# TensorE signals once in each attention step, at the scores, instead of several times; ten buffers for the one-hot matrices instead of six

## What is computed

```python
s_i = relu(einsum('bthd,bsd->bths', q_i, k_i))       # 4 index heads
I = einsum('bths,h->bts', s_i, idx_w)
I = where(local, inf, I); I = where(causal, -inf, I)   # the last 64 keys always
_, idx = top_k(I, 96)
key_c, value, kr_sel = ...[bi, idx]                    # 96 keys for each query
scores = (q_c . key_c + q_r . key_r) * scale           # 8 heads
out = softmax(scores) . value @ W_out
```

## Time and profile before

| what | us |
| --- | --- |
| median of three timed runs (939.28 to 943.36) | 941.9 |
| span of the profiled execution | 1199.2 |
| TensorE busy in the span | 913.6 |
| VectorE busy | 679.3 |
| ScalarE busy | 509.0 |
| GpSimd busy | 480.2 |
| chain that ended last: TensorE / another core or unknown queue / VectorE / issue / ScalarE | 46% / 20% / 13% / 10% / 8% |

### The profile page before, as it was taken

The page is one execution under the profiler, slowest core; times in us unless marked ns, Lnnn a source line. Parts: engine busy times, 40 slices in busy tenths (PEclk is TensorE's granted clock), DMA queues, the critical chain, the costliest instruction groups (busy, mean ns, idle before and its releaser), DMA issues.

```text
span 1199.2 us, 17728 instructions
## 1 busy us (share of the span) xinstructions
PE 913.6 (76%) x5742; PEld 520.4 (43%) x5742; DVE 679.3 (57%) x1979; ACT 509.0 (42%) x1463; POOL 480.2 (40%) x738
## 2 busy tenths in 40 slices
PE   6699749289479796879676794875749897888885
PEld 3345415145245453536343352443426582343353
DVE  3788628067158466549474473884403314968763
ACT  5456315044136464547354372643416332423420
POOL 3600562712711777573717427156560104411020
PEclk8668859679579788879687697885859998988987
DMA  8101211101100111110101001001070251000000
GB/s 232 34 1 25 43 26 38 29 20 33 29 19 5 25 26 23 21 23 16 23 11 22 19 12 23 11 17 25 16 188 21 69 139 31 1 1 10 0 10 18
DMA packets 59642, 39.98 MB, mean 33 GB/s; under 512 B 27072, under 2 KB 51360, under 8 KB 59424
## 3 DMA queue, kind: packets, MB, share of 16 engines
q1 hardware_dynamic: 44064, 23.40, 7.6%
q0 software_dynamic: 12800, 14.15, 5.8%
q10 hardware_dynamic: 2688, 1.31, 0.4%
HBM read 33.31 MB, written 5.55 MB: 32 GB/s over the span
## 4 chain that ended last, share of the span: by engine, by line
PE 46%; another core or an unknown queue 20%; DVE 13%; issue 10%; ACT 8%; DMA 1%; POOL 1%; SPq 0%; DVEq 0%; ACTq 0%; POOLq 0%
PE psI L655 5%; PE psK L745 5%; PE psK L641 4%; PE psS L1753 3%; PE psP L807 3%; PE psP L814 2%; PE psS L781 2%; PE psK L733 2%; ACT R L903 2%; PE psP L796 2%; PE psS L784 2%; DVE SC L1115 2%; PE psP L641 2%; DVE G L1971 1%
## 5 line engine op out<-in xcount | busy, mean ns | idle before, releaser
L621 POOL DMA_INDIRECT G<-key_rows,idx x284 | 276.2, 973 | 349.0 <-DVEq L1142 247.8
L1031 ACT ACTIVATE PT<-psP 128x256 f32<-128x256 f32 x128 | 48.7, 380 | 360.1 <-remote 270.3
L1311 DVE CUSTOM_DVE_ANT_0 S<-psS,cst 128x208 f32<-128x208 f32 x128 | 47.4, 370 | 262.9 <-remote 225.2
L655 PE MATMUL psI<-kiT,qiT 64*128 64x512 f32 (+5 forms) x320 | 108.3, 697 | 74.1 <-ACT R L903 57.1
L641 PE MATMUL psK<-cst 128*128 128x512 bf16 x315 | 101.4, 437 | 6.3 <-issue 6.3
L781 PE MATMUL psS<-KT,Q 96*32 96x128 f32 x1024 | 64.8, 305 | 27.9 <-remote 17.5
L1115 DVE SCALAR_TENSOR_TENSOR SC<-R,w_i,SC 128x512 f32<-128x512 f32 (+5 forms) x120 | 78.5, 654 | 5.5 <-ACT R L903 1.9
L1145 DVE MAX8 top<-SC 128x8 f32<-128x128 f32 (+15 forms) x64 | 78.5, 1226 | 2.3
L1007 ACT ACTIVATE KT<-psK 96x512 f32<-96x512 f32 x96 | 56.7, 591 | 51.9 <-remote 26.4
L903 ACT ACTIVATE R<-psI 128x512 f32<-128x512 f32 (+5 forms) x160 | 73.3, 510 | 12.2 <-PE psI L655 6.0
L1147 DVE FIND_INDEX8 idxf<-top,SC 128x8 uint32<-128x128 f32 (+15 forms) x64 | 78.2, 1223 | 0.0
(11 more groups left out here) (348 smaller groups left out, 1889.1 us busy)
## 6 DMA issues: line engine op xcount, KB each, us to landing
G<-key_rows,idx POOLq DMA_INDIRECT x284
rtmp<-idx_rows SPq DMA_DIRECT2D x32, 128.0 KB
xslots<-zrow SPq DMA_DIRECT2D x4, 320.0 KB, 9.0
SC<-xslots SPq DMA_DIRECT2D x8, 160.0 KB
yslots<-SC ACTq DMA_DIRECT2D x8, 160.0 KB, 2.7
V<-val_rows SPq DMA_DIRECT2D x15, 80.0 KB
xr<-in_x SPq DMA_DIRECT2D x1, 1024.0 KB, 9.3
qiT<-in_w_gate SPq DMA_DIRECT2D x4, 256.0 KB
```

Source lines behind the costliest of these rows:

```text
L621: pool.indirect_dma_start(ring[o % RING][:, g % GPB, DR:], None, key_rows, bass.IndirectOffsetOnAxis(ap=idx[:, t, g:g + 1], axis=0),).then ...
L655: pe.matmul(psI[i][:, 0:w], lhs, kiT[64 * i:64 * i + 64, CH * c:CH * c + w], start=True, stop=True).then_inc(s["i_mm"], 1)
```

## The change

One semaphore, `pe_step`, takes the place of thirteen in the loop. TensorE raises it once a step, on the last matmul of `scores(n-1)` (or of `out_project`, where a step has one). `through(n)` is the count after step n, and all readers on ScalarE, VectorE, GpSimd and SyncE wait for the count of the step in which their matmuls stand. What stood at the end of a step (`tail`: index pair, query, router) now runs at the start of the next one, after the signal, and is covered by the signal of that next step. `out_project(t)` moves from ahead of the scores of step 8(t+2) to the end of step 8(t+2)-1, and waits for `s_min` and `vs_cp` there in place of the wait for `s_y_mm`. `one_hot` gets four more buffers, in the half of `ot_region` that `OT` leaves free, and `key_match` waits once a block, for the end of the step of the block before the last, not for single key tiles.

```diff
-NVS, NOH = 7, 6
+NVS, NOH = 7, 10
...
+        def tail_of(n):
+
+            return (n in index_pairs or n in Q_AT or n in QT_AT or n == LAST_Y
+                    or any(n in TILE_AT[stage] for stage in ("x1_t", "router", "cumulate")))
+
+        counted = [n for n in range(N0, N1 + 1) if tail_of(n - 1) or 0 <= n < NT * NB + LAG_W]
+
+        def through(n):
+
+            return sum(1 for m in counted if m <= n)
...
-                    if b == NB - 1 and t >= 1:
-                        out_project(t - 1)
-                        pe.wait_ge(s["y_mm"], t)
...
-                for n in range(N0, N1):
-                    st, b = divmod(n, NB)
-                    keep_warm(psK, WARM_TAIL.get(n - NT * NB, 0))
+                for n in range(N0, N1 + 1):
+                    mm = tail(n - 1)
+                    if n < N1:
+                        keep_warm(psK, WARM_TAIL.get(n - NT * NB, 0))
                     if 0 <= n - LAG_T < NT * NB:
-                        p_transpose(n - LAG_T)
+                        mm = p_transpose(n - LAG_T)
                     if 0 <= n - LAG_W < NT * NB:
-                        weighted(n - LAG_W)
+                        mm = weighted(n - LAG_W)
                     if n == 1:
                         rank_transpose()
                     if 0 <= n < NT * NB:
-                        front(n)
+                        mm = front(n)
                     if 0 <= n - LAG_S < NT * NB:
-                        scores(n - LAG_S)
+                        mm = scores(n - LAG_S)
+                    if n in Y_AT:
+                        pe.wait_ge(s["s_min"], n - 1)
+                        if (n - 4) // NB in ONE_HOT:
+                            pe.wait_ge(s["vs_cp"], hot_order(n - 4) + 1)
+                        mm = out_project(Y_AT[n])
+                    if n in counted:
+                        mm.then_inc(s["pe_step"], 1)
...
                 def k_copy(n):
                     if n // NB in ONE_HOT:
                         return
-                    act.wait_ge(s["k_t"], ring_order(n) + 1)
-                    if n >= 2:
-                        act.wait_ge(s["s_mm"], n - 1)
+                    act.wait_ge(s["pe_step"], through(n))
...
                 def p_copy(n):
-                    act.wait_ge(s["p_t"], n + 1)
-                    if n >= 1:
-                        act.wait_ge(s["pv"], n)
+                    act.wait_ge(s["pe_step"], through(n + LAG_T))
...
                 def o_copy(n):
                     t, b = divmod(n, NB)
-                    act.wait_ge(s["pv"], n + 1)
+                    act.wait_ge(s["pe_step"], through(n + LAG_W))
...
+                    if m >= 2:
+                        dve.wait_ge(s["pe_step"], through(hot_block[m - 2]))
                     for kt in range(key_tiles(n)):
                         o = hot_tiles(n) + kt
-                        if o >= NOH:
-                            dve.wait_ge(s["oh_mm"], o - NOH + 1)
...
                 def key_rank(n):
 
-                    dve.wait_ge(s["oh_mm"], hot_tiles(n + 1))
+                    dve.wait_ge(s["pe_step"], through(n))
...
                 def s_minimum(n):
                     t, b = divmod(n, NB)
-                    dve.wait_ge(s["s_mm"], n + 1)
+                    dve.wait_ge(s["pe_step"], through(n + LAG_S))
```

More of the change, by code:

```diff
@@ L654, in index_pair @@
                         lhs = qiT[64 * i:64 * i + 64, pair, P * t:P * (t + 1)]
-                        pe.matmul(psI[i][:, 0:w], lhs, kiT[64 * i:64 * i + 64, CH * c:CH * c + w],
-                                  start=True, stop=True).then_inc(s["i_mm"], 1)
+                        mm = pe.matmul(psI[i][:, 0:w], lhs, kiT[64 * i:64 * i + 64, CH * c:CH * c + w],
+                                       start=True, stop=True)
+                    return mm
                 pe.wait_ge(s["ld_w"], 16 * 7)
@@ L707, in q_project @@
                         pe.wait_ge(s["q_cp"], 2 * t)
-                    pe.matmul(psM[:, :], cqT[:, P * t:P * (t + 1)], w_q[:, :], start=True,
-                              stop=True).then_inc(s["q_mm"], 1)
+                    return pe.matmul(psM[:, :], cqT[:, P * t:P * (t + 1)], w_q[:, :], start=True, stop=True)
                 def q_transpose(t, j):
@@ L843, in cumulate, with tail @@
                               skip_group_check=True)
-                    pe.matmul(PX[:, E0:2 * E0], ones, ohsum[:, :], start=False, stop=True,
-                              skip_group_check=True).then_inc(s["cum_mm"], 1)
-                for n in range(N0, N1):
-                    st, b = divmod(n, NB)
-                    keep_warm(psK, WARM_TAIL.get(n - NT * NB, 0))
+                    return pe.matmul(PX[:, E0:2 * E0], ones, ohsum[:, :], start=False, stop=True,
+                                     skip_group_check=True)
+                def tail(n):
+                    mm = None
+                    for t, u in index_pairs.get(n, ()):
+                        mm = index_pair(t, u)
+                    if n in QT_AT:
+                        mm = q_transpose(*QT_AT[n])
+                    if n in Q_AT:
+                        mm = q_project(Q_AT[n])
+                    if n == LAST_Y:
+                        mm = out_project(NT - 1)
+                    if n in TILE_AT["x1_t"]:
+                        mm = x1_transpose(TILE_AT["x1_t"][n])
+                    if n in TILE_AT["router"]:
+                        mm = router(TILE_AT["router"][n])
+                    if n in TILE_AT["cumulate"]:
+                        mm = cumulate(TILE_AT["cumulate"][n])
+                    return mm
+                for n in range(N0, N1 + 1):
+                    mm = tail(n - 1)
+                    if n < N1:
+                        keep_warm(psK, WARM_TAIL.get(n - NT * NB, 0))
                     if 0 <= n - LAG_T < NT * NB:
-                        p_transpose(n - LAG_T)
+                        mm = p_transpose(n - LAG_T)
                     if 0 <= n - LAG_W < NT * NB:
-                        weighted(n - LAG_W)
+                        mm = weighted(n - LAG_W)
                     if n == 1:
@@ L1339, in route @@
                 def route(t):
-                    dve.wait_ge(s["lg_mm"], t + 1)
+                    dve.wait_ge(s["pe_step"], through(stage_step("router", t) + 1))
                     if t >= 1:
```

119 lines of the change are left out of this document (56 added, 63 removed).

## The result

The changed kernel takes 1083.8 us (median of 4 runs, 1079.5 to 1088.3), the kernel before 942.1 us beside it: ratio 1.151, interval [1.147, 1.156]. That is 142 us more, where I had forecast 96. The profiled execution of the change has a span of 1084.6 us, as long as its timed runs, so this profile, unlike that of before, can stand for them.

What follows compares the result with a forecast made beforehand. The prediction took TensorE to bound the timed kernel, with GpSimd's gathers close behind. It summed 941.9 + 126 of added waits - 30 of room = 1038 us (ends 1014 and 1068), with a range of 968 to 1090.

Steps and rivals of the forecast that it cites:

- The bare step: Step of the last tile without an index pair: near 3.7 us in the change instead of 2.84.
- the wait of a chained pair: TensorE, before an index pair following a step with one, waits 1.93 us for ReLUs; extra 1.5 us each.
- the clock's rival: TensorE idles, a sixth of the steps fall to 1.2 GHz: +53 us, 1090; chance 0.16.
- the own wait: TensorE's wait on its own s_y_mm in scores() goes: about 0.2 us, 15 times, -3 us.
- The last tile: Eight steps at the attention loop's end: near 33 us in the change instead of 27.5, TensorE no longer full.
- it stays near 28 us: Sign against the forecast: the last tile keeping its length would mean the timed run's bound was not TensorE.
- The room: Slack TensorE has today in the attention loop, taking back 30 us of the added waits, between 0 and 54.
- the price of 5.46 us a block: GpSimd's four gathers of a block, 131.11 to 136.57 in tile 5; 64 blocks taken as 350 us.
- the gathers' rival: Gathers bind the timed run more and cover the waits: only about 38 us counts, 980; chance 0.14.
- The added waits: ScalarE's copies start only after the step's scores, so TensorE waits: +126 us on its path, summed by kind of step.
- Against: the waits are short, and the index pair or the warm matmuls lie between them: Argument on TensorE against the granted clock falling to 1.2 GHz in a sixth of the steps, +53 us.
- The late signals: TensorE signals long after their matmuls, 311 us of profiled delay, at most about 54 timed; as rival 915, chance 0.10.

Runs made afterwards that it cites:

- hold: The kernel before with all its signals, plus one wait: p_copy also waits for the scores at the end of its step; 1089.4 us, 1.160.
- pv: The changed kernel with one signal a step put back, on the last matmul of weighted(), for p_copy and o_copy; 1011.9 us, 1.069.
- pvim: The changed kernel with two signals put back: weighted()'s for p_copy and o_copy, and each index pair's for the ReLUs; 955.0 us, 1.014.
- more: The kernel before with 896 more TensorE signals, seven a step, read by nobody; 942.9 us, 1.0017.
- slim10: The kernel before without some 300 signals and with ten one-hot buffers, no copy waiting for the step's end; 942.8 us, 1.0015.
- slim10_nospace: The kernel before without some 300 signals, with ten one-hot buffers and without GpSimd's spacer memsets between gathers; 898.5 us, 0.954.
- the second profile: The kernel before, unchanged, profiled once more; 943.9 us, span 941.9.
- a_nospace: The changed kernel without GpSimd's spacer memsets between gathers; 1074.7 us, 1.141.
- warm6: The changed kernel with six short warm matmuls at the start of each step with an index pair right after a step with one; 1091.8 us, 1.159.

## Why the prediction was right, and where its sizes were off

*Right: the sign, the place and the mechanism.* `p_copy` starts as the scores end, TensorE waits for it and, in chained steps, for the ReLUs. The bare step is 3.77 us as foretold (3.7; before, give 2.83, where I wrote 2.84), and the wait of a chained pair 1.90 (1.93). `hold`, `pv` and `pvim` show that this serialisation is the cause. The time is within the range. But it is outside the ends of my own sum (1014 and 1068): that it lies inside is owed to the clock's rival, which set the upper end.

*Right: fewer signals and more buffers gain next to nothing.* `more`, `slim10` and `slim10_nospace` show it. The -3 us for the own wait was never tested alone, and moving `out_project` isn't free: in `pvim` it stood 11.5 us in its new place.

*The last tile.* I expected near 33 us; it took 36.5, with 7.82 in step 127, where TensorE also waits for a gather. Before, it isn't quiet as in the first profile (27.5 us) but takes 43.4, since gathers hold it. So the sign "it stays near 28 us" rested on a reading that the timed run doesn't share.

*The room, 30 us.* It is right in size, by luck: I took about the middle between 0 and 54 because the rows decided no further. Its owner is one that I had named only as a part: gathers, in the last 24 steps. They took 130.3 us before and 99.4 in the change, 31 back. What I had wrong is the price of 5.46 us a block, read from the first block of tile 5. In the second profile the gathers of tile 8 begin at 278.54, after a pause of 7.55 us for the indices, and the last gather of all at 664.12, so 64 blocks took 387 us, 6.04 each, and not 350. From step 43 to step 127 the kernel before takes 392 us, as long as they do: their lead lasts up to step 104, and afterwards they are late. Against the gathers' rival, my 84 steps at 5.0 us are then 33 us more than 64 blocks, not 70; that comparison, which is of the changed kernel, still holds, as `a_nospace` shows.

*The added waits, 126 us: the term that was mis-sized.* By the spans, what was added measured 173 (142 and the 31 of the room). The steps 6 to 103 came to 170 us more, and those ahead of step 6 to 7 more. My prices for the steps 7 to 103 sum to 47 x 1.5 + 17 x 1.2 + 16 x 0.6 = 100 us, measured 168. The idle time that was added, 92 us, is nearly what I had priced, and in the two steps shown at full clock so are the prices: bare 0.94 (0.85 before cover, of which I took off 0.25 for tails that cover less), chained 1.64 (1.5). What I had left out of the sum is the **granted clock**: it fell from 0.99 to 0.87 and 0.86 in these stretches, and the same matmuls were busy for 78 us more. I take most of these 78 as its price, an estimate from the windows, since ends of matmuls in a profile are modelled; what an experiment gave back is 31 us in the gather tiles (`warm6`). The failed step is "Against: the waits are short, and the index pair or the warm matmuls lie between them". I had the clock only in a rival, at 0.16, whose 1090 is my 1038 and 53 for the clock. That rival, and not my forecast, describes the result: waits and clock hold at once, at 1084. Its 53 came from a guess (a sixth of the steps).

*The late signals.* They were rightly kept out of the timed run. But I tied their beginning to that of the gathers, and the second profile has the same gathers and no such delay: they are that one execution's, and no later profile had them again. Their cause stays open.

The sum against the spans: +7 before step 6, +170 up to step 104, -31 from there to step 127, -4 after it, 142 in all.

## What to carry to other kernels

A signal is not a cost to save for its own sake: 896 more of them changed nothing, while one copy that waited for the end of a step instead of its own matmuls, with the queue behind it, cost 15%. When signals are merged, write down for each reader what it runs beside now and who waits for it. Add the clock to the sum, since here TensorE's matmuls got longer once waits entered most steps. And where an engine works through its queue in order, an earlier signal helps a reader only if everything ahead of it in the queue is free too. Before you work on the engine that binds most of the time, look whether another stretch has another bound: the small spacers of GpSimd, in the 24 steps that gathers bind, were worth 42 us.

## What the runs showed of the hardware that I had not expected

- With some 1 to 2 us of waiting in most steps, TensorE's granted clock goes from 0.99 to 0.87, and the same two matmuls after the same 1.90 us wait take 1.13 us in one step and 1.76 in the next. Six short warm matmuls in the wait of the chained steps brought it from 0.86 to 0.96 in steps 40 to 103.
- A memset of 0.17 us between two indirect gathers costs 0.13 to 0.42 us of the queue's time (1.25 us from gather to gather without it, 1.38 to 1.67 with it).
- One profiled execution can be a quarter longer than all others of the same program (1199 against 942 us), with waits of up to 31.5 us for TensorE signals. A second profile of the same kernel, beside the timed median, is the test.
